# Edge rows' two halves side by side in four banks of sums, and another order around an expert's sums

## The reference

```python
xn = layernorm(x)
# relations: mean over the edges of one relation into one node
msg  = xn[src] * edge_weight[:, None]
h    = segment_sum(msg, edge_type * N + dst) / maximum(count, 1)
gnn  = einsum('rnc,rco->no', h.reshape(8, N, C), weight) + xn @ root + bias
# linear attention over all nodes, 8 heads of 32, feature map elu(.) + 1
mix  = (q @ (k^T v) / (q . sum(k) + 1e-6)) @ wo + bo
x    = x + gnn + mix
# six experts of three layers 256 -> 256 -> 256 -> 256, the best two of a router
f    = layernorm(x)
p    = softmax(relu(f @ router_w1 + b1) @ router_w2 + b2); two best, softmax of the two
x    = x + sum over the two of weight * expert(f)
```

## Time and profile before

| | us |
|---|---|
| median of 3 runs | 3180.59 |
| lowest and highest | 3175.07, 3182.59 |
| span of the profiled execution | 3900.9 |

### The profile page before, as it was taken

The page is one execution under the profiler, slowest core; times in us unless marked ns, Lnnn a source line. Parts: engine busy times, 40 slices in busy tenths (PEclk is TensorE's granted clock), DMA queues, the critical chain, the costliest instruction groups (busy, mean ns, idle before and its releaser), DMA issues.

```text
span 3900.9 us, 48061 instructions
## 1 busy us (share of the span) xinstructions
PE 3132.7 (80%) x16807; PEld 2709.1 (69%) x16808; DVE 2360.3 (61%) x5405; ACT 2004.5 (51%) x3996; POOL 1638.6 (42%) x1696
## 2 busy tenths in 40 slices
PE   6999999766878778777777777787787778787788
PEld 5888887656767767666666667676676667677677
DVE  4497552246666667566666656666565666666675
ACT  3555555334555555454555555555555455545564
POOL 0000000145555555554555555554545455555540
PEclk9999999888888888888889888888888889898899
DMA  6665555543233333233323333233323333233320
GB/s 242 250 259 196 210 210 212 224 144 112 84 93 95 99 96 94 82 94 91 90 77 96 95 92 89 85 97 89 92 83 91 90 93 91 79 97 93 100 67 11
DMA packets 179841, 456.72 MB, mean 117 GB/s; under 512 B 46604, under 2 KB 104918, under 8 KB 159405
## 3 DMA queue, kind: packets, MB, share of 16 engines
q0 software_dynamic: 80352, 219.14, 19.5%
q1 hardware_dynamic: 97074, 232.64, 16.5%
q10 hardware_dynamic: 2172, 1.85, 0.1%
HBM read 296.01 MB, written 158.29 MB: 116 GB/s over the span
## 4 chain that ended last, share of the span: by engine, by line
PE 41%; another core or an unknown queue 12%; DVE 10%; ACT 10%; issue 7%; DVEq 1%; DMA 0%; SPq 0%; ACTq 0%
PE bank L1655 27%; PE acc L1709 7%; DVE row_lo L1394 4%; ACT row_hi L1216 4%; ACT bank L1231 3%; ACT h_hi L1230 2%; PE acc L1718 1%; PE bank L1793 1%; PE bank L1682 1%; PE bank L1691 1%; PE acc L1655 1%; DVE y L1540 1%; DVE h_lo L1473 1%; DVE sel L1388 1%
## 5 line engine op out<-in xcount | busy, mean ns | idle before, releaser
L1159 POOL DMA_INDIRECT ring<-y_tab,tab x1666 | 1624.1, 975 | 1401.6 <-PE acc L1709 869.9
L1230 ACT ACTIVATE h_hi<-bank,bias_t 128x512 fp32r<-128x512 f32 (+1 forms) x600 | 408.9, 682 | 1078.1 <-remote 565.1
L1709 PE MATMUL acc<-row_hi,sel 128*128 128x256 f32 x1666 | 501.6, 329 | 446.5 <-DVE row_lo L1394 255.5
L1709 PEld LDWEIGHTS acc<-row_hi,sel 128*128 128x128 f32 x1666 | 369.9, 222 | 508.3 <-DVE row_lo L1394 291.1
L1216 ACT ACTIVATE row_hi<-ring,tab 128x256 fp32r<-128x256 f32 x1666 | 704.1, 510 | 31.4 <-PE acc L1709 19.4
L1394 DVE SCALAR_TENSOR_TENSOR row_lo<-ring,tab,row_hi 128x256 fp32r<-128x256 f32 x1666 | 685.1, 479 | 48.9 <-ACT row_hi L1216 34.4
L1473 DVE TENSOR_TENSOR h_lo<-bank,h_hi 128x512 fp32r<-128x512 f32 (+1 forms) x600 | 392.6, 676 | 447.2 <-ACT bank L1231 360.5
L790 PE MATMUL yb<-wr_hi,xhl 128*128 128x512 f32 x1568 | 510.9, 398 | 31.5 <-ACT yst L351 25.4
L1655 PE MATMUL bank<-ew_hi,h_hi 128*128 128x256 f32 x1176 | 384.2, 327 | 179.0 <-DVE h_lo L1473 177.7
L1709 PE MATMUL acc<-row_lo,sel 128*128 128x256 f32 x1666 | 480.9, 315 | 13.4 <-issue 13.2
L1540 DVE SCALAR_TENSOR_TENSOR y<-bank,gate,y 128x256 f32<-128x256 f32 x490 | 213.0, 479 | 349.7 <-PE bank L1655 227.7
(11 more groups left out here) (272 smaller groups left out, 5219.7 us busy)
## 6 DMA issues: line engine op xcount, KB each, us to landing
y_tab<-yst SPq DMA_DIRECT2D x97, 1024.0 KB, 3.9
ring<-y_tab,tab POOLq DMA_INDIRECT x1666
xt_tab<-xhl SPq DMA_DIRECT2D x25, 1024.0 KB, 3.9
xc<-xt_tab SPq DMA_DIRECT2D x25, 1024.0 KB
x<-x_tab SPq DMA_DIRECT2D x49, 256.0 KB
xs<-in_x SPq DMA_DIRECT2D x24, 512.0 KB, 6.0
x_tab<-xs SPq DMA_DIRECT2D x24, 512.0 KB, 5.0
out<-y SPq DMA_DIRECT2D x24, 512.0 KB
```

The lines of the kernel that those rows point to most:

```text
L1159: pool.indirect_dma_start(out=out_ap, out_offset=None, in_=y_tab[:, :], in_offset=bass.IndirectOffsetOnAxis(ap=idx_ap, axis=0)).then_inc(s ...
L1230: act.activation(dest[:, m, 0:W], b[:, 0:W], ACT.Relu, bias=bias)
L1709: last = pe.matmul(sums(t), sel[:, p % BUFS, q, :], half, start=False, stop=False, skip_group_check=True)
```

## The change

- `halves` replaces row_hi and row_lo: a tile's high and low rows side by side, 512 columns, two buffers. `aggregate` has one product of 512 columns a tile, so that a node tile's sum has a high and a low half of 256 columns in a bank of its own; acc takes four banks, and four instead of five are left for the items. The ramp in PSUM goes; `one_hot` reads iota_w in SBUF.
- `root` does the same: one product with [high, low] of the weights side by side and one with the low features.
- The ring has 4 slots, freed by `lo_ready` (low rows made) instead of portion_used.
- DVE adds the two halves of the sums to x1 in two passes (`sums_and_statistics`), and does it, with the statistics, in the iteration before, ahead of the last expert's y sums; PE's close_sum stands ahead of w3(5).
- PE takes two portions ahead of w3 in experts 1 to 4 and none behind h2. DVE forms one portion's low rows ahead of the y sums, takes all y sums together, and prepares a second portion behind them (`SPLIT_AT`). ACT splits whole portions at the expert's end.
- b3 and the gates are split in fp32r parts, stacked in 96 rows, so that four single-pass products give b3's term.

```diff
-SLOTS, BUFS = 6, 2
+SLOTS, BUFS = 4, 2
+GROWS, GH = 96, 32
-AHEAD_W3 = {0: 3, 1: 4, 2: 6, 3: 8, 4: 10, 5: 11}
-BEHIND_H2 = {2: 5, 3: 7, 4: 9}
+AHEAD_W3 = {0: (2,), 1: (3, 4), 2: (5, 6), 3: (7, 8), 4: (9, 10), 5: (11,)}
+SPLIT_AT = {0: (3, 4), 1: (5, 6), 2: (7, 8), 3: (9, 10), 4: (11, PARTS), 5: (PARTS + 1,)}
...
+            halves = sbuf(pc, "halves", [P, BUFS, PT, 2, C], F32R)
+            hot_r = sbuf(pc, "hot_r", [P, BUFS, PT, NT], F32R)
-            acc = psum(pc, "acc", (P, SUB * C))
-            NBANK = 5
+            acc = psum(pc, "acc", (P, SUB * 2 * C))
+            acc_parts = acc[:, :].rearrange("p (t h c) -> p t h c", t=SUB, h=2)
+            NBANK = 4
-            ramp = psum(pc, "ramp")
...
 # POOL, portion
-                    pool.wait_ge(portion_used, portions_before(n, p) - SLOTS + 1)
+                    if nth_portion(n, p) >= SLOTS:
+                        pool.wait_ge(lo_ready, nth_portion(n, p) - SLOTS + 1)
...
 # DVE, gates
+                    for h in range(2):
+                        dve.tensor_copy(gate3[:, 0:T, h * GH:h * GH + 8], gate[:, 0:T, :])
+                    dve.drain()
+                    dve.tensor_tensor(gate3[:, 0:T, 2 * GH:2 * GH + 8], gate[:, 0:T, :], gate3[:, 0:T, 0:8].bitcast(F32),
+                                      ALU.subtract).then_inc(gate_ready, 1)
...
 # DVE, the sums, ahead of the last expert's y sums
+                        dve.tensor_tensor(x1[:, two, :], acc_parts[:, two, 0, :], x1[:, two, :], ALU.add)
+                        dve.drain()
+                        dve.tensor_tensor(x1[:, two, :], acc_parts[:, two, 1, :], x1[:, two, :], ALU.add).then_inc(x1_done, 1)
...
 # DVE, expert e (between the low halves and the y sums)
+                        if coming:
+                            one_hot(i + 1, coming[0])
+                        if len(coming) == 2:
+                            low_rows(i + 1, coming[0])
+                        if e == EXPERTS - 1 and more:
+                            sums_and_statistics(i + 1, tiles(LOOP if i + 1 < SUPER - 1 else LAST_ONE))
...
+                        if len(coming) == 2:
+                            prepare(i + 1, coming[1])
...
 # PE
-                        for half in (row_hi[:, p % BUFS, q, :], row_lo[:, p % SLOTS, q, :]):
-                            last = pe.matmul(sums(t), sel[:, p % BUFS, q, :], half, start=False, stop=False,
-                                             skip_group_check=True)
+                        last = pe.matmul(sums(t), hot_r[:, p % BUFS, q, :], halves[:, p % BUFS, q, :, :], start=False, stop=False,
+                                         skip_group_check=True)
...
+                        for p in AHEAD_W3[e] if more else ():
+                            aggregate(i + 1, p)
+                        if more and e == EXPERTS - 1:
+                            close_sum(i, plan)
```

More of the change, by code:

```diff
@@ L1261, in iteration @@
                         if e == 1:
[L1262 to L1268 removed]
+                            gone(act.activation(gate_t[:, 0:W], take(i, plan, "gt", 0)[0:GROWS, 0:W], ACT.Copy))
+                        for p in SPLIT_AT[e] if more else ():
+                            high(i + 1, p)
                 act.dma_start(wo_sb[:, :, :], wo.rearrange("(k p) n -> p k n", p=P)).then_inc(small_c, 16)
@@ L1455, in gates @@
                     dve.drain()
[L1456 to L1457 removed]
+                    dve.tensor_tensor(gate[:, 0:T, :], hot[:, 0, 0:T, :], hot[:, 1, 0:T, :], ALU.add)
                     dve.drain()
[L1460 to L1476 removed]
@@ L1496, in iteration, with low @@
                     last.then_inc(xn_c, 1)
+                def iteration(i, plan):
+                    T = tiles(plan)
+                    W = T * NT
+                    more = plan is LOOP
+                    def low(kind, e):
+                        if e == EXPERTS:
+                            return
+                        hi, lo_ = (h1_hi, h1_lo) if kind == "h1" else (h2_hi, h2_lo)
+                        for m in range(KC):
+                            dve.wait_ge(h_set, nth_hidden(i, kind, e, m) + 1)
+                            gone(dve.tensor_tensor(lo_[:, m, 0:W], bank[plan[kind, (e, m)][0]][:, 0:W],
+                                                   hi[:, m, 0:W].bitcast(F32), ALU.subtract))
+                    scales(i, T)
                     if more:
-                        low_rows(i + 1, 1)
                         query_features(i, plan)
@@ L1505, in iteration @@
                     if more:
-                        prepare(i + 1, 2)
+                        low_rows(i + 1, 1)
                     low("h1", 0)
@@ L1509, in iteration @@
                     if more:
-                        prepare(i + 1, 3)
+                        prepare(i + 1, 2)
                     for e in range(EXPERTS):
-                        second = AHEAD_W3[e] if more and e in BEHIND_H2 and AHEAD_W3[e] < parts(i + 1) else None
-                        low("h2", e, second)
-                        if second is not None:
-                            low_rows(i + 1, second)
+                        coming = SPLIT_AT[e] if more else ()
+                        low("h2", e)
                         if e == 0:
@@ L1535, in iteration @@
                         for h in range(T // 2):
-                            if h == 1 and coming is not None and e + 1 in BEHIND_H2:
-                                low_rows(i + 1, coming)
                             b = take(i, plan, "w3", (e, h))
```

176 lines of the change are left out of this document (78 added, 98 removed).

## The result

| | us |
|---|---|
| after, median of 6 runs (lowest, highest) | 3202.97 (3195.10, 3210.73) |
| before beside it, median of 6 | 3177.83 (3173.00, 3187.24) |
| ratio after / before, 95% interval | 1.0066 [1.0044, 1.0089] |

The change makes the kernel 25 us slower. 3188 had been forecast.

A forecast was written before the change was run, and what follows sets the result against it. PE was taken as the bound, 83.4 of 91.3 us an iteration. Work -2.0, stalls +2.2 and one_hot +0.25 gave +0.45 x 24 = +11, less 4 once: 3180.6 to 3188 us; range 3100 to 3265, the forecast's own 3160 to 3215.

The forecast's parts named there:

- PE's work, -2.0: Each iteration on PE: edges save 0.5 us, root 0.1, b3 1.4; together -2.0, PE at 81.4.
- The low rows' waits go: PE's waits for second portions in experts 2, 3 and 4, about 1.9, 0.9 and 1.9 us, disappear.
- Four banks: PE waits for banks or low halves at h1(2) 2.4 us, the denominators 1.8 and h2(2) 2.3.
- the layout: Engines' orders laid out by undisturbed distances over one iteration: PE's stalls 7.0 us after against 5.5 before.
- The scaling by 1.44: Real stalls exceed the layout's by 7.9/5.5 = 1.44 in both kernels: 10.1 against 7.9, +2.2 us an iteration.
- The clock, 0 in the forecast: PE's granted clock stays 1.00 across the new gaps of 2 us each, so no cost was added.
- Rival 2: Slower: h1(2)'s gap grows towards 4 us and half clock costs about 3 an iteration, 3260 us; chance 0.22.
- The last iteration, -4: Last turn: close_sum ahead of a third layer covers the statistics, saving some 3 to 4 us once.
- One_hot from SBUF, +0.25: DVE's selection matrix compared from SBUF: +0.25 us an iteration in front of stalls, 0 where DVE isn't awaited.
- POOL, a floor of 87: POOL's gathers need about 87 us an iteration, with 3 to 5 us idle; cost 0.
- rival 3: Slower: POOL as bound, one_hot from SBUF holding back gathers, 3 us on 87 make 90; 3210 us; chance 0.12.
- Rival 1: Faster: bank gaps are small; 3129 us if PE's stalls stay at 7.9, 3071 if only 5.5; chance 0.26.

The follow-up runs named there:

- e1: The kernel before, unchanged, recorded a second time for a cleaner trace: 3176.06 us.
- e4: After, with b3 and the gates left in float32 and the split gates' DVE operations gone: 3177.92 us, 0.9991 of before.
- e8: After, with the first group's high rows made by ACT in two pieces of three, as before the change: 3197.52 us, 1.0051 of before.
- e3: Before, with the selection matrix compared from iota_w in SBUF instead of the ramp in PSUM: 3182.41 us, 1.000 of before.
- e11: After, with e7's order, portion 5 split before the gates' copy, e8's pieces, selections directly ahead of low rows, and b3 in float32: 3130.21 us, 0.9830 of before.
- e6: After, with DVE taking expert 0's y sums ahead of portion 3's selection matrix and low rows: 3247.64 us, 1.0215 of before.
- e7: e6, with DVE also preparing portion 4 behind the low halves of h2(1) instead of ahead: 3152.36 us, 0.9916 of before.

## Why the prediction was right or wrong, point by point

**What bounds the kernel.** Right that 720 us were the recording's and that pitches in undisturbed stretches hold: PE's work comes to 83.2 us an iteration, predicted 83.4. Wrong in the iteration's length: 91.3 took 946.6 for the first sums, and that number was itself delayed by the recording. In e1 and in after the single lines read, sums of e1 first:

```profile
L1479 DVE TENSOR_TENSOR x<-acc,x x49: 671/679/693, 901.8 to 3130.6; 128x512 f32<-128x512 f32 x49
```

```profile
L1480 DVE TENSOR_TENSOR x<-acc,x x49: 672/675/687, 914.3 to 3161.3; 128x512 f32<-128x512 f32 x49
```

(3130.6 - 901.8) / 24 = 92.9. The 2.4 us "I can't place" were therefore 4.4 in e1's terms: 0.6 ahead of w3(5), 1.9 in gaps under 0.3 us, and 1.9 of half clock.

**PE's work, -2.0:** measured 81.3 - 83.2 = -1.9. Nearly right in its terms: 512 columns at 0.232, b3 at 4 x 0.12 or so; e4, which undoes b3, gives 1.2 back where 1.4 were forecast, and edges and root saved 0.7 where 0.6 were.

By the formula for an isolated product under "Back-to-back issue gap" in the Trainium skill's "TensorE: Matmul & The Clock Gate", edges and root would have given 0.2, an estimate. The trace disagrees: e4 has 0.7 less than before with b3 equal (82.5 for 83.2), so the distances of the rows decide.

**The low rows' waits go:** right. In after no portion behind the first waits for low rows as long as 0.1 us on the mean.

**Four banks:** right in place and nearly in size. On the means: h1(2) 2.5 (laid out 2.4), denominators 1.2 (1.8; it is 1.6 in ten iterations of 15 and absent in the five with the clock down), h2(2) 2.7 (2.3), router 0.5 (0.5), and 0.7 ahead of the turn, which the layout had as none; 7.65 for 7.0. Even the clock times hold: with zero at 1957.3, h1(2) starts at 24.0 (24.3), the denominators at 28.7 (28.8); h2(2) starts at 41.4 (39.5), behind products at half clock that the layout does not have.

**The scaling by 1.44:** wrong. Stalls of both kernels were supposed to exceed the layout in one ratio, +2.2. Measured are 8.9 against 8.3, +0.6: what the layout leaves out is not in proportion to it.

**The clock, 0 in the forecast:** the term of the sum that failed, and the clock's fall in each iteration was on the prediction's own list of signs that it is wrong. "Granted clock 1.00 across them" rested on one row behind a gap of 2.27. Half clock costs 1.9 us an iteration before and 4.0 after, +2.1, as much as the whole saving on PE. In each of iterations 5 to 19 of after the clock is down, for about 10 us on the mean, and in before for about 4.5. Rival 2 had the mechanism and 3 us as its price, but tied it to a gap that grows "towards 4 us"; it came with gaps of 2.2, 1.6 and 2.6 as they were laid out. The runs of after go the same way: the fastest has a mean granted clock of 0.955 (3195.1 us) and the slowest 0.949 (3210.7).

**The sum of an iteration:** -1.9 + 0.6 + 2.1 = +0.8 against the forecast's +0.45; x 24 some +19 for +11. That this comes so close is luck: the stalls were put 1.6 too high, by the factor of 1.44, the one_hot term 0.25 too high, and the clock 2.1 too low, and the errors all but cancel. The path was right (banks freed late by DVE against a saving on PE), the account of what the gaps cost was not. The forecast of the whole, 7 us over before, became 25, and most of that difference lies outside the iterations.

**The last iteration, -4:** wrong. PE's timeline of the last turn, after and then before:

```profile
3159.19 3.62 PE L1737 MATMUL acc<-kw_sb,qf 128*128 128x256 f32 x16
...
3167.82 0.63 PE L1719 MATMUL bank<-ident,xn_c 128*128 128x128 f32 x4 [2.17 <-DVE xn_c L1496]
```

```profile
3128.26 3.98 PE L1718 MATMUL acc<-kw_sb,qf 128*128 128x256 f32 x16
...
3133.96 0.63 PE L1701 MATMUL bank<-ident,xn_c 128*128 128x128 f32 x4 [1.72 <-DVE xn_c L1494]
```

The gap is 2.2 instead of 1.7. The third layer does cover the statistics, but the last y sums now stand on DVE between them and the scaled rows, and they wait for that third layer.

**What I left out:** the first group. It costs 13.5 us, two thirds of what all iterations cost, and stood in the kernel: `high` lost its two pieces there. e8 gives 10 of it back in the trace; the other 3 stay open.

**One_hot from SBUF, +0.25:** its own duration is the same (946 and 949 ns for six tiles in e1 and e3), and e3 costs nothing in time. The other end of that term, POOL, is where it acts.

**POOL, a floor of 87:** 87 holds for the old ramp (86.6 in e1), but with the new one it is 91.0; rival 3's 3 us for the ramp, 90, was the better number (e3 alone: 89.5). It did not decide after, where POOL still waits 3.0 us of each iteration, so rival 3 did not come true. But it decides what can be had of after: 94.2 - 91.0 = 3.2 us an iteration or 77 us, as long as POOL's line stays (90.6 to 92.1 in the runs here), and the best kernel here, e11, is 73 us below after.

**Rival 1, faster:** its premise, small bank gaps, is false. Its number, 3129, was reached by e11 (3130), with other orders and b3 in float32.

## What to carry to other kernels

A change that trims PE's work and adds gaps of 2 us can pay twice, in the gap and in the clock behind it; price the clock from many gaps, not from one row. When a wait is taken out of a hand-written order, follow the same engine to its next customer first (e6 lost 45 us, e7 with one more step gained 51). And read the engine that never waits: once POOL's slack of 3 us was used up, further changes of order mostly moved the stall.

## What was not expected of the hardware

- The clock fell behind a gap of 1.87 us in e1 (0.72 over the 3 us that follow), and stayed at 1.00 behind one of 2.19 in after, while 1.61 shortly behind that one, and 2.59 by itself, gave 0.50. Over 15 iterations of after, gaps of 2.18 to 2.56 ahead of h1(2) were followed by a fall five times, and gaps of 2.19 to 2.74 ten times not. No single length of gap separates the two here.
- A DVE operation of 0.95 us that reads its ramp from SBUF instead of PSUM is no slower itself and makes POOL's gathers 41 ns longer on the mean (982 to 1023), 2.8 us a group; those that run beside it alone grow from 963 to 1117.
- A recording can delay one stage of a kernel (946.6 for 901.8) while distances in undisturbed stretches agree with those of a clean trace (b3's eight pieces 1.92 us in both, PE's work 83.4 and 83.2).
